# Decoder layers on one core: an engine-by-engine order written out for all eight batches, and a new order of the first loads

## The reference, cut to what matters

```python
x = x + _L0_attn_ref(_layernorm(x), Wq, Wk, Wv, Wo)             # stage a
x = x + _L0_xattn_ref(_layernorm(x), ctx, ctx, gates ...)       # stage b: mLSTM cell
x = x + _L0_ffn_ref(_layernorm(x), ...)                         # stage c: top-k routing, expert rows, plus an MLP
x = x + _L1_attn_ref(_layernorm(x), Wk, Wq, Wv)                 # stage d: causal attention
x = x + _L1_xattn_ref(_layernorm(x), ctx, mask, Wq, Wk, Wv, Wo) # stage e: pooled cross attention with a mask
x = x + _L1_ffn_ref(x, ...)                                     # six local-attention blocks
```

## Time and profile before

| | us |
|---|---|
| median of 3 runs | 3901.14 (3901.01 to 3903.59) |
| the profiled execution | 3898.82 |
| its span, first to last instruction | 3897.1 |
| so around the span | 1.7 |
| first layers, within the span | 0 to about 937 |
| local-attention blocks | about 937 to 3897 |

### The profile page before, as it was taken

How to read it: one execution, slowest core, us unless ns; L and a number is a source line. 1 busy time by engine, 2 the same in 40 slices (tenths; PEclk the granted TensorE clock), 3 DMA queues, 4 the chain that set the end, 5 groups by cost and what they waited for, 6 DMA issues and landing times.

```text
span 3897.1 us, 78634 instructions
## 1 busy us (share of the span) xinstructions
PE 3680.6 (94%) x27016; PEld 2612.3 (67%) x27016; DVE 2758.1 (71%) x9072; ACT 2306.5 (59%) x6802; POOL 2239.6 (57%) x2099
## 2 busy tenths in 40 slices
PE   6899998965799999999999999999999999999997
PEld 4566666643467777777777777677777776777776
DVE  2688888753677777777777777777777777777763
ACT  2355554432566676666666766666667666666663
POOL 1677777763665556556556565565565655655640
PEclk7899999987899999999999999999999999999999
DMA  3777777881000010000000000100100001000000
GB/s 124 159 182 186 184 183 186 180 219 43 1 7 7 4 40 17 28 7 17 28 17 27 7 29 15 33 12 7 40 15 22 14 4 40 15 30 7 4 7 28
DMA packets 111065, 211.64 MB, mean 54 GB/s; under 512 B 22320, under 2 KB 72016, under 8 KB 109136
## 3 DMA queue, kind: packets, MB, share of 16 engines
q0 software_dynamic: 40960, 134.25, 14.3%
q1 hardware_dynamic: 69568, 72.24, 5.8%
q10 hardware_dynamic: 144, 0.13, 0.0%
HBM read 191.92 MB, written 2.10 MB: 50 GB/s over the span
## 4 chain that ended last, share of the span: by engine, by line
PE 70%; issue 2%; DVE 1%; POOL 1%; ACT 1%; DMA 0%; SPq 0%; DVEq 0%; POOLq 0%; ACTq 0%
PE pj L1657 24%; PE pj L1737 12%; PE y_ps L1720 8%; PE y_ps L1746 6%; PE sc L1685 5%; PE tp L1696 5%; PE o_ps L1711 5%; PE tp L1665 4%; PE tp L1635 1%; POOL l_qk_rot L1598 1%; ACT l_probs L1816 0%; DVE l_probs L1953 0%; POOL l_r_k L1603 0%; POOL l_r_q L1603 0%; DVE l_qk_cos L1929 0%
## 5 line engine op out<-in xcount | busy, mean ns | idle before, releaser
L1657 PE MATMUL pj<-w_qkv,l_xT 128*128 128x512 f32 x2304 | 1065.7, 599 | 5.5 <-DMA l_qk_gain<-in_gains 3.3
L1598 POOL TENSOR_TENSOR l_qk_rot<-l_qk_cos,l_qk_sin 128x512 f32<-128x512 f32 x384 | 564.8, 1471 | 842.2 <-DVE l_qk_sin L1932 556.5
L1657 PEld LDWEIGHTS pj<-w_qkv,l_xT 128*128 128x128 f32 x2304 | 414.7, 192 | 385.8 <-issue 376.9
L405 POOL DMA_INDIRECT f_rows<-in_emb,f_expert x512 | 508.3, 993 | 236.3 <-issue 145.8
L1816 ACT ACTIVATE l_probs<-l_probs,l_low 128x128 f32<-128x128 f32 x1536 | 594.1, 391 | 2.1 <-DVE l_low L1953 0.4
L1737 PE MATMUL pj<-l_xnT,l_w 128*128 128x256 f32 x2112 | 511.7, 388 | 2.2 <-issue 1.2
L1924 DVE TENSOR_REDUCE l_ss<-l_qk_sq 128x8 f32<-128x512 f32 x384 | 261.7, 681 | 326.5 <-ACT l_qk_sq L1803 174.9
L1781 ACT ACTIVATE l_qk_raw<-pj 128x512 f32<-128x512 f32 x384 | 227.2, 592 | 435.6 <-PE pj L1657 422.1
L1953 DVE CUSTOM_DVE_ANT_0 l_probs<-sc,l_shut,l_r_q 128x128 f32<-128x128 f32 x1536 | 440.4, 344 | 55.0 <-PE tp L1696 46.7
L1737 PEld LDWEIGHTS pj<-l_xnT,l_w 128*128 128x128 f32 x2112 | 384.5, 191 | 65.2 <-issue 17.4
L1720 PE MATMUL y_ps<-w_o,l_oT 128*128 128x256 f32 x1536 | 341.2, 380 | 3.5 <-ACT l_oT L1781 3.5
(11 more groups left out here) (335 smaller groups left out, 6890.8 us busy)
## 6 DMA issues: line engine op xcount, KB each, us to landing
w_qkv<-in_L_ffn_Wqkv SPq DMA_DIRECT2D x12, 1024.0 KB, 6.9
l_w<-in_ff_w SPq DMA_DIRECT2D x6, 1408.0 KB, 6.0
f_rows<-in_emb,f_expert POOLq DMA_INDIRECT x512
w_o<-in_L_ffn_Wo SPq DMA_DIRECT2D x6, 1024.0 KB, 5.6
w_qkv<-in_L_ffn_Wqkv SPq DMA_DIRECT2D x12, 512.0 KB, 4.8
l_xf<-l_stream SPq DMA_DIRECT2D x48, 128.0 KB
l_xf<-l_stream SPq DMA_DIRECT2D x48, 127.0 KB
l_w<-in_ff_w SPq DMA_DIRECT2D x6, 768.0 KB, 4.7
```

The source lines that it names most:

```text
L405: pool.indirect_dma_start(rows[:, j % RH, k, :], None, dram["emb"], bass.IndirectOffsetOnAxis(ap=expert[:, n % 2, at:at + 1], axis=0)).the ...
L1598: pool.tensor_tensor(qk_rot[:, i % ROTS, :], qk_cos[:, b, :], qk_sin[:, b, :], ALU.add).then_inc(rotated if s == 0 else pool_front, 1)
L1657: last = pe.matmul(pj[b][:, :], xT[:, k, t * P:(t + 1) * P], w_qkv[:, k, s * INNER + c * 512:s * INNER + (c + 1) * 512], start=(k == 0), s ...
```

## The change

The five tables with offsets become five lists that name the batch of every piece. The pieces and their counts are the same; their order differs on each engine, most in the first and the last batches. On SP, x of batch 1 is loaded ahead of batch 0's context, x of batch 2 where x of batch 1 was, and `e_mask.0` is issued right after the first loads and `e_ctx.0`. On POOL, the tables that the first pieces need are filled first, then the first root `a_rstd.0` runs, then the rest (`start_later`).

```diff
-    ORDER["vector"] = [
-        ("c_s0", -4), ("c_s1", -4), ("c_s2", -4), ("c_coef11", -5), ("c_dot12", -5), ("c_s3", -4), ("c_dot13", -5), ("c_pair", -4), ("c_coef12", -5),
...
+    ORDER["vector"] = """
+        a_stats.0 a_shift.0 a_stats.1 e_mask.0 a_shift.1 a_z.0 a_probs.0 a_y.0 b_stats.0 b_shift.0 a_stats.2 a_z.1 a_shift.2 b_g.0 a_probs.1 b_scan.0
...
+    ORDER["sync"] = """
+        e_ctx.0 b_ctx.0 e_mask.0 b_ctx.1 b_ctx.2 b_ctx.3 e_ctx.1 e_mask.1 e_ctx.2 b_ctx.4 e_mask.2 b_ctx.5 e_mask.3 e_ctx.3 e_mask.4 e_ctx.4 b_ctx.6
...
     def pieces(engine):
-        for step in range(-FIRST, BATCH + LAST):
-            for piece, ahead in ORDER[engine]:
-                if 0 <= step + ahead < BATCH:
-                    yield piece, step + ahead
+        for event in ORDER[engine]:
+            piece, n = event.split(".")
+            yield piece, int(n)
...
             sp.wait_ge(consts_set, 1)
+            load_x(1)
             b_ctx(0)
...
-            load_x(1)
+            load_x(2)
...
-            for n in range(2, BATCH):
+            for n in range(3, BATCH):
                 load_x(n)
...
                 pool.sem_inc(consts_set, 1)
+                pool.iota(iota8[:, :], pattern=[[1, TOPK]], base=0, channel_multiplier=0, allow_small_or_imprecise_dtypes=True).then_inc(set_step, 1)
+                made[0] += 1
+                fill(zeros[:, :], 0.0)
+                fill(pooled[:, KC, :], 0.0)
+                fill(e_o[:, 8 * NB:9 * NB], 0.0)
                 fill(block_mask[:, :, :], 0.0)
...
+            def start_later(pool):
                 fill(head_row[:, :, :], 1.0)
...
             start(pool)
-            for piece, n in pieces("gpsimd"):
+            for at, (piece, n) in enumerate(pieces("gpsimd")):
                 do[piece](n)
+                if at == 0:
+                    start_later(pool)
```

More of the change, by code:

```diff
@@ L60, in first_layers @@
     ORDER = {}
-    ORDER["tensor"] = [
[3 rows of a table removed]
-        ("c_fold", -5), ("c_y0", -4), ("c_up0", -4), ("d_hT", -5), ("a_o", -2), ("d_q", -5), ("c_up1", -4), ("d_k", -5), ("d_v", -5), ("a_y", -2),
[3 rows of a table removed]
-        ("c_up8", -4), ("c_hT", -3), ("e_y", -5), ("e_u", -5), ("c_q1", -3),
-    ]
-    ORDER["scalar"] = [
-        ("c_hT", -4), ("c_tanh9", -5), ("c_tanh10", -5), ("c_diag9", -5), ("c_q1", -4), ("c_q0", -4), ("c_diag10", -5), ("a_hT", -2),
-        ("c_tanh11", -5), ("b_cT", -3), ("c_diag11", -5), ("c_tanh12", -5), ("b_norm", -3), ("a_q", -2), ("e_k", -5), ("a_k", -2), ("c_diag12", -5),
-        ("c_tanh13", -5), ("b_hT", -3), ("a_v", -2), ("c_diag13", -5), ("c_mtanh0", -4), ("c_tanh14", -5), ("c_diag14", -5), ("c_tanh15", -5),
-        ("a_exp", -2), ("c_exp", -4), ("c_diag15", -5), ("c_fold", -5), ("c_tanh0", -4), ("c_diag0", -4), ("c_mtanh1", -4), ("d_norm", -5),
-        ("c_tanh1", -4), ("d_hT", -5), ("c_diag1", -4), ("b_ln", -3), ("a_o", -2), ("c_tanh2", -4), ("a_norm", -1), ("d_k", -5), ("d_q", -5),
-        ("b_low", -3), ("c_diag2", -4), ("d_v", -5), ("c_tanh3", -4), ("d_exp", -5), ("d_pT", -5), ("c_diag3", -4), ("c_tanh4", -4), ("b_m0", -3),
-        ("b_m1", -3), ("c_diag4", -4), ("b_m2", -3), ("c_tanh5", -4), ("e_norm", -5), ("b_m3", -3), ("e_v", -5), ("c_tanh6", -4), ("c_diag5", -4),
-        ("e_w", -5), ("e_q", -5), ("c_diag6", -4), ("b_sq", -3), ("e_exp", -5), ("c_tanh7", -4), ("c_tanh8", -4), ("e_pT", -5), ("c_diag7", -4),
-        ("c_diag8", -4), ("e_cT", -4), ("c_norm", -3), ("e_o", -5), ("e_y", -5),
-    ]
```

167 lines of the change are left out of this document (141 added, 26 removed), and 12 rows, old and new, of the table ORDER.

## The result

The changed kernel takes 3920.5 us (median of 5 runs, 3919.5 to 3925.5), against 3901.0 for the kernel before, measured with it: a ratio of 1.0052, 95% interval 1.0041 to 1.0064. It is 0.5% slower. The forecast was 3900.5 with a range of 3886 to 3914; the result lies 20 us above the forecast and outside the range.

The account below looks back on a forecast made before the run. Batch 0's dependent chain bounds the start, PE and POOL nearly the 96.8 us per batch behind it; 15.4 - 9 - 4 - 3 = -0.6 gives 3898.2 profiled, plus 2.3 for the median: 3900.5 us, range 3886 to 3914.

Parts of the forecast that it names:

- The mask: Start: VectorE waits for batch 0's mask, landing at 38.7 us; x after stage a and first gather 15.4 us later.
- the gains of the start: First layer norm and loads of x: a_rstd.0 some 4.5 us sooner, worth nothing behind the longer mask wait.
- The low clock behind the long wait: PE after the mask wait: costed at 0; as a rival, clock stays low, +5.7 us, 3906.2, chance 0.03.
- Batch 0's gathers beside batch 1's stage b: First to second routing: b.1's heads ahead of c_up fill PE's waits, -9 us, 6 of it by the second routing.
- the 3 us of work done ahead: Part of the -9: PE does a_k.3, a_q.3, a_v.3 and e_k.0 inside former waits, 3 us.
- The middle batches: Five batches: new lists fill PE's waits ahead of e_o and e_u, half of 7.9 gained, -4 us, ends +4 and -12.
- the mark at which it would be wrong: Middle batches: prediction is wrong if their period moves by more than 1.5 us.
- waits for DMAs: Slower rival: e_ctx.1 and e_ctx.5 behind a whole b_ctx, 5 us waits at several places, 3911, chance 0.05.
- The end: Last batch: POOL's 9.3 us wait for c_up, a third gained, -3 us, ends 0 and -9.
- What follows the first layers: Everything behind the first 937 us: costs the same before and after, 0.

Follow-up runs that it names:

- e13: Old lists with the change's new start, but TensorE's c_up8 of the batch before behind c_hT in six batches: 3912.0 us, 1.0025 to the kernel before.
- e5: The changed kernel with its lists kept, but batch 0's mask transfer issued right behind x 0, ahead of all weights: 3896.2 us, 0.9985 to the kernel before.

## Why the prediction was wrong

**The mask** was right: landing at 38.9 (38.7 forecast), `a_exp.0` at 41.21 (41.2), x after stage a 49.22 - 35.05 = 14.2 us later (15.4), the first routing 12.2 us later. What it did not say is that this 12.2 is a loss of 25.6 over a gain of 13.4. The prediction set the gains of the start to nothing because a later wait swallowed them, which holds for the sum, but it took the rest of the way to the first gather to be unchanged. It is 2.0 us shorter even behind the mask (75.0 against 77.0 us from the addition of stage a to the first routing), and up to 9.7 us of the new lists show once the wait is gone (5.4 against the 104.0 of e13). The low clock behind the long wait, put at no more than before, was no more: PE worked 30.7 us at the low level ahead of the first routing, and 33.6 in the kernel before.

**Batch 0's gathers beside batch 1's stage b**, -9: the second routing came 90.2 us after the first (88 to 92 forecast), with 6 us of gain by then as written. The path was right: `b_h1.1` ended 37.6 us after the first routing (41 forecast, 47.3 before) and `c_hT.1` started 59.3 us after it (57 to 59 forecast, 64.9 before). Where PE's time came from was wrong, so that the size is right partly by luck. PE was to use its former waits; its idle time is 17.0 us after and 17.2 before. The 5.9 us are busy time, 73.2 against 78.9, at a clock of 0.91 against 0.82: the low level lasted 16 us in place of 34. And the 3 us of work done ahead did not show: the next pitch was 102.6 against 98.6.

**The middle batches**, -4 with ends of +4 and -12, is the step that failed. It measured +14.5 in five batches, and +18.5 with the pitch before them, 22.5 us off the forecast where the total missed by 20. That is 2.9 us a batch, and the prediction had named 1.5 as the mark at which it would be wrong. The step took the waits of the earlier trace rows, saw that the new lists put work into them, and counted half of them as gained. The waits did go. But ahead of `c_hT` PE's list isn't what sets a batch: the way from `b_h1` over VectorE, POOL and ScalarE to `f_hc` is as long as before (88.9 us in five batches against 88.0), so PE, which has less left to do there, waits at `c_hT` for what it saved. A wait filled ahead of a fixed date is not a gain. That the sum then rose was not priced at all. Behind `c_hT` it rose by 3.9 us: in batches 5 to 7 the waits had joined into one of 3.8 to 6.3 us, with the fall of the clock behind it (24.8 us of PE's busy time at the low level there, 11.2 before; 17.2 or more in every unfilled trace with the new middle, 11.2 or less with the old one, e13 aside), and `c_up8` stood on the chain (e13). Between the routing and `b_h1`, where PE does nearly nothing but work, it rose by 9.7: by the clock records 5.1 for the clock, 1.2 idle, and 3.3 of work at full speed that the new lists do ahead of `b_h1`. No run took this larger part by itself. Nor is all of it sure to come: e5, with the same middle lists, had no more low clock in PE's busy time than the kernel before (31.9 and 31.2 us) and took 489.8, so some 7 us come with the order at an equal clock, and the rest, 9.0 of the 14.5 in this pair of traces by the clock records, varies from execution to execution. The prediction did price a low clock, as 5.7 us once at the start. It had in the earlier trace rows a clock of 0.96 in the middle and 0.82 before, and did not ask what the new order does to it in every batch. No rival had the middle longer but by waits for DMAs; one such wait came, 3.4 us ahead of `e_cT.1` between the second and the third routing.

**The end**, -3: +1.1. POOL's 9.3 us of waiting for `c_up` became 3.1, and the last gather started 87.1 us after the eighth routing in place of 90.8. But `c_fold.7` came 18.0 us after that gather and not 12.7; the new order has pieces of the batch before ahead of `c_up12.7` to `c_up15.7`. Gained and given back in the same stage. What follows the first layers was 4.2 us shorter, forecast at 0; the low clock there was 53 us against 61, and half of that difference is 4.

What stays open is which entries of VectorE's and ScalarE's new lists make `c_diag8` and `f_hc` late together, which work moved ahead of `b_h1`, and why one list gave 489.8 to 498.6 us for the same five batches in different executions. PE's idle time in these traces is nearly the same (41.8 to 43.7 us), and its busy time at the low level goes from 31.9 to 52.5 us with the length, so the difference is the clock; but what starts it each time isn't shown.

## What to carry to other kernels

A piece with a wait for a transfer belongs behind all that can run without it: 1 us of work hoisted to the head of an in-order engine cost 19 to 26 us here, and issuing its transfer second and not behind 26 others made it free (e5). When a new order fills an engine's small waits, look for the next date that it doesn't set itself; if the chain to that date is as long as before, the waits are only collected there. Such a wait can be free by itself and still cost here, since the clock falls behind it, on the chain (e13). So cut a loss at the dates that other engines set, and see in which part it lies. Compare the same stretch by length, idle time, busy time and granted clock: the four together say whether a loss is waiting, work or clock, where each of them alone misled.
